# Down and output tiles of a transformer layer: two half-width passes in place of two half sums

## Time and profile before

| | |
|---|---|
| time, 3 runs | 985.96, 980.02, 984.0 us; median 984.0 us |
| the profiled execution | 981.32 us, its span 979.6 us |
| busy share of the span | PE 92%, weight loads 62%, DVE 60%, ACT 51%, POOL 33% |
| mean granted clock of TensorE | 0.978 of full |
| the chain that ended last | PE 80%, DVE 10%, ACT 5%, DMA 3% |
| matmuls of `split_product` (L987) | 984 |

### The profile page before, as it was taken

The page is one execution under the profiler, slowest core; times in us unless marked ns, Lnnn a source line. Parts: engine busy times, 40 slices in busy tenths (PEclk is TensorE's granted clock), DMA queues, the critical chain, the costliest instruction groups (busy, mean ns, idle before and its releaser), DMA issues.

```text
span 979.6 us, 19130 instructions
## 1 busy us (share of the span) xinstructions
PE 902.2 (92%) x7091; PEld 608.4 (62%) x7091; DVE 589.7 (60%) x1681; ACT 498.5 (51%) x998; POOL 319.3 (33%) x320
## 2 busy tenths in 40 slices
PE   2797999999999999999999999988989899989985
PEld 2665666666766666666666666554666566555764
DVE  7765666666666666666666666677576776621134
ACT  2432556565655555555555565566455454445110
POOL 4032234352525252525252535250212222211035
PEclk8899999999999999999999999999999999989998
DMA  9466242424242433333333334356747363335644
GB/s 293 132 191 206 64 137 80 132 87 130 88 127 92 120 98 108 105 108 106 105 106 104 113 99 131 102 143 201 195 121 207 104 188 110 106 94 162 193 135 150
DMA packets 142938, 129.08 MB, mean 132 GB/s; under 512 B 36176, under 2 KB 104368, under 8 KB 142624
## 3 DMA queue, kind: packets, MB, share of 16 engines
q1 hardware_dynamic: 142848, 127.87, 44.4%
HBM read 74.07 MB, written 53.22 MB: 130 GB/s over the span
## 4 chain that ended last, share of the span: by engine, by line
PE 80%; DVE 10%; ACT 5%; DMA 3%; issue 2%; POOL 1%; SPq 0%; POOLq 0%; DVEq 0%; ACTq 0%
PE bank L959 25%; PE bank L987 12%; PE o L1115 12%; PE s L1079 9%; PE st L1098 7%; PE bank L260 4%; PE bank L261 3%; PE bank L262 3%; DVE junk L1611 2%; PE bank L921 2%; DVE neg_pad L1627 1%; PE bank L934 1%; PE bank L938 1%; DMA inv_sums<-scratch_r 1%; ACT prob L1368 1%
## 5 line engine op out<-in xcount | busy, mean ns | idle before, releaser
L1368 ACT ACTIVATE prob<-st 128x512 f32<-128x512 f32 (+1 forms) x640 | 324.8, 554 | 262.7 <-PE st L1098 262.2
L1611 DVE CUSTOM_DVE_ANT_0 junk<-s,mask 128x128 bf16<-128x128 f32 (+3 forms) x512 | 229.2, 487 | 111.1 <-PE s L1079 110.9
L1614 DVE TENSOR_REDUCE part_max<-s 128x1 f32<-128x512 f32 x256 | 163.9, 682 | 96.0 <-PE s L1079 96.0
L1079 PE MATMUL s<-k,q 64*128 64x512 f32 (+3 forms) x768 | 151.7, 381 | 15.1 <-DVE part_max L1611 11.9
L527 POOL TENSOR_SCALAR_AFFINE_SELECT prob<-prob 128x512 f32<-128x512 f32 x128 | 83.4, 664 | 227.1 <-ACT prob L1368 226.6
L959 PE MATMUL bank<-x_hi,w_hi 64*128 64x512 f32 (+1 forms) x704 | 150.7, 415 | 2.4 <-DVE hid L1477 1.1
L1115 PE MATMUL o<-prob,v 128*32 128x512 f32 (+3 forms) x1536 | 145.4, 497 | 0.0
L1098 PE MATMUL st<-q,k 64*128 64x512 f32 (+3 forms) x768 | 130.5, 356 | 13.0 <-ACT prob L1368 12.9
L959 PE MATMUL bank<-x_lo,w_hi 64*128 64x512 f32 (+1 forms) x704 | 142.4, 391 | 0.0
L959 PE MATMUL bank<-x_hi,w_lo 64*128 64x512 f32 (+1 forms) x704 | 141.8, 389 | 0.0
L1079 PEld LDWEIGHTS s<-k,q 64*128 64x128 f32 x768 | 78.2, 185 | 61.7 <-DVE part_max L1611 32.0
(11 more groups left out here) (140 smaller groups left out, 1065.8 us busy)
## 6 DMA issues: line engine op xcount, KB each, us to landing
hid_in<-scratch_hid SPq DMA_DIRECT2D x16, 1408.0 KB, 7.2
q<-scratch_q SPq DMA_DIRECT2D x60, 200.0 KB
scratch_hid<-tanh_hid_hi SPq DMA_DIRECT2D x40, 256.0 KB, 2.1
scratch_hid<-hid_lo SPq DMA_DIRECT2D x40, 256.0 KB, 2.4
scratch_o<-o_sb SPq DMA_DIRECT2D x32, 256.0 KB
scratch_q<-proj_hi SPq DMA_DIRECT2D x30, 256.0 KB
k<-scratch_k SPq DMA_DIRECT2D x30, 192.0 KB
ctx<-scratch_o SPq DMA_DIRECT2D x16, 256.0 KB, 3.9
```

The costliest lines, as they stand in the source:

```text
L1079: pe.matmul(sb_[(p + odd) % S_BANKS][:, 0:wd], q[half, g % 2, h // 2, qt * P:(qt + 1) * P], k[half, g % 2, k0:k0 + wd], start=True, stop=T ...
L1368: nc.scalar.activation(prob[:, job % 3, h, 0:JOB_COLS[j]], st[at % ST_BANKS][:, 0:JOB_COLS[j]], ACT.Exp, scale=float(HD) ** -0.5).then_inc ...
L1611: ins = dve.tensor_tensor_reduce(junk[:, n % S_BANKS, 0:wd], bank_[:, 0:wd], mask[:, C - wd:C], 1.0, LOWEST, ALU.add, ALU.max, part[:, h, ...
L1614: ins = dve.tensor_reduce(part[:, h, qt, dst:dst + 1], bank_[:, 0:wd], AX.X, ALU.max)
```

## The change

Down 0 to 11 and out 0 to 7 no longer make half sums. In a first pass the upper 64 rows of the factors compute the left 256 columns into bank 0 while the lower 64 rows compute the right 256 columns into bank 1; then PE waits for its own first pass (`crossed`), and in the second pass the upper rows add their part to the right columns in bank 1 and the lower rows theirs to the left columns in bank 0. Each bank then holds finished columns. For a down tile that is 132 matmuls of 256 columns, each with a weight load of 128 columns, where there were 66 of 512; for an output tile 48 where there were 24.

The 12 steps of a down tile are now all used: five of two blocks and one of one block in the first pass, one of one and five of two in the second; `filled` comes in the 12th. ACT copies the right 256 columns of y and DVE the left 256; they stand after 12 steps. `tanh_y` and `gate_y` stand one step later in the output tile that follows. ACT no longer copies for an output tile; `combine` adds the bias straight from the two banks, in two instructions of 256 columns, and waits for `r2_done` of the tile before.

```diff
+COLUMNS = [slice(0, D // 2), slice(D // 2, D)]
+DOWN_STEPS = [[list(range(h, min(h + 2, NH))) for h in range(0, NH, 2)],
+              [list(range(max(h, 0), h + 2)) for h in range(-1, NH, 2)]]
+OUT_STEPS = [[[0, 1], [2, 3]]] * 2
...
+            def changing_over(key, factors, steps):
+                for cross in range(2):
+                    if cross:
+                        pe.wait_ge(crossed, CROSSED[key])
+                    for step in steps[cross]:
+                        for n in step:
+                            for m, (lhs, rhs) in enumerate(factors(n)):
+                                for odd in range(2):
+                                    i, half = odd ^ cross, head_rows(odd, HALF_ROWS)
+                                    mm = pe.matmul(bank[i][:, COLUMNS[i]], lhs[half], rhs[half, COLUMNS[i]],
+                                                   start=not cross and n == 0 and m == 0,
+                                                   stop=cross == 1 and n == steps[cross][-1][-1] and m == 2)
+                        if step is steps[cross][-1]:
+                            mm.then_inc(filled if cross else crossed, 1)
+                        yield 1
...
-            def copy_half_y(t):
+            def copy_right_y(t):
                 wait_filled(act, ("down", t, 0))
                 if t:
                     act.wait_ge(y_done, t)
-                nc.scalar.activation(yb[:, :], bank[1][:, :], ACT.Copy).then_inc(y_half, 1)
+                nc.scalar.activation(yb[:, COLUMNS[1]], bank[1][:, COLUMNS[1]], ACT.Copy).then_inc(y_right, 1)
...
-            def copy_half_out(t):
-                wait_filled(act, ("out", t, 0))
-                if t:
-                    act.wait_ge(r2_done, t)
-                nc.scalar.activation(r1[:, :], bank[1][:, :], ACT.Copy).then_inc(r_half, 1)
...
-            def add_half_y(t):
-                dve.wait_ge(y_half, t + 1)
-                dve.tensor_tensor(yb[:, :], bank[0][:, :], yb[:, :], ALU.add).then_inc(y_sum, 1)
+            def copy_left_y(t):
+                wait_filled(dve, ("down", t, 0))
+                if t:
+                    dve.wait_ge(y_done, t)
+                dve.tensor_copy(yb[:, COLUMNS[0]], bank[0][:, COLUMNS[0]]).then_inc(y_left, 1)
...
                 if t < SPLIT_OUT:
-                    dve.wait_ge(r_half, t + 1)
-                    dve.tensor_tensor(r1[:, :], bank[0][:, :], r1[:, :], ALU.add).then_inc(r1_done, 1)
-                    dve.wait_ge(r1_done, t + 1)
-                    dve.tensor_tensor(r1[:, :], r1[:, :], bias[:, :], ALU.add).then_inc(r_bias, 1)
-                    dve.wait_ge(r_bias, t + 1)
+                    for i, read in enumerate((r_left, r1_done)):
+                        dve.tensor_tensor(r1[:, COLUMNS[i]], bank[i][:, COLUMNS[i]], bias[:, COLUMNS[i]], ALU.add).then_inc(read, 1)
+                    dve.wait_ge(r_left, t + 1)
...
@@ ACT and DVE: where the pieces stand @@
-                        yield NH - ROUND_AT
+                        yield STEPS["down"] - ROUND_AT
-                    yield STEPS["down"] - NH
                     if 1 <= t <= NT // 2:
-                        yield 1
+                        yield 2
                         tanh_y(t)
-                        yield STEPS["out"] - 1
-                        copy_half_out(t - 1)
+                        yield STEPS["out"] - 2
...
-                        yield 2
+                        yield 3
                         gate_y(t)
-                        yield STEPS["out"] - 2
+                        yield STEPS["out"] - 3
                         combine(t - 1)
```

More of the change, by code:

```diff
@@ L203 @@
 BANKS, PRIOR = bank_places()
+CROSSED = {key: n + 1 for n, key in enumerate(key for key in BANKS if len(BANKS[key]) == 2)}
 def interleave(attention, background, background_first=False):
@@ L413, in layer @@
         d_zero = sem("d_zero")
[L414 to L417, removed]
+        y_right = sem("y_right")
+        y_left = sem("y_left")
+        r_left = sem("r_left")
         yt_done = sem("yt_done")
@@ L470, in read_out @@
             if kind == "down" and a < SPLIT_DOWN:
-                return (y_half, a + 1), (y_sum, a + 1)
+                return (y_left, a + 1), (y_right, a + 1)
             if kind == "out" and a < SPLIT_OUT:
-                return (r_half, a + 1), (r1_done, a + 1)
+                return (r_left, a + 1), (r1_done, a + 1)
             if kind == "hidden":
@@ L952, in hidden @@
                     if cross:
-                        pe.wait_ge(crossed, NCH * h + c + 1)
+                        pe.wait_ge(crossed, CROSSED["hidden", h, c])
                     for kt in range(KT):
@@ L996, in down @@
                 out_ = take_bank(("down", t, 0))
+                if t < SPLIT_DOWN:
+                    hi, lo = (hin[:, t % 2, j] for j in range(2))
+                    yield from changing_over(
+                        ("down", t, 0), lambda h: [(hi[:, h], dh[:, h]), (hi[:, h], dl[:, h]), (lo[:, h], dh[:, h])], DOWN_STEPS)
+                    return
                 for h in range(NH):
                     hi, lo = (hin[:, t % 2, j, h] for j in range(2))
[L999 to L1002, removed]
+                    mm = matmul_hi_lo(pe, out_[:, :], hi, lo, dh[:, h], dl[:, h], h == 0, h == NH - 1)
                     if h == NH - 1:
@@ L1011, in output @@
                 out_ = take_bank(("out", t, 0))
+                if t < SPLIT_OUT:
+                    hi, lo = ch[:, t % 3], cl[:, t % 3]
+                    yield from changing_over(
+                        ("out", t, 0), lambda kb: [(hi[:, kb], woh[:, kb]), (hi[:, kb], wol[:, kb]), (lo[:, kb], woh[:, kb])], OUT_STEPS)
+                    return
                 for kb in range(KT):
                     hi, lo = ch[:, t % 3, kb], cl[:, t % 3, kb]
[L1014 to L1017, removed]
+                    mm = matmul_hi_lo(pe, out_[:, :], hi, lo, woh[:, kb], wol[:, kb], kb == 0, kb == KT - 1)
                     if kb == KT - 1:
@@ L1239, in tanh_y @@
                 if t < SPLIT_DOWN:
-                    act.wait_ge(y_sum, t + 1)
+                    act.wait_ge(y_left, t + 1)
+                    act.wait_ge(y_right, t + 1)
                 else:
@@ L1332, in background @@
                             split_wo(kb)
-                        yield NH - KT * WO_STEPS
+                        yield STEPS["down"] - KT * WO_STEPS
                     else:
@@ L1340, in background @@
                             split_context(context_beside(t))
-                        yield NH - ROUND_AT
+                        yield STEPS["down"] - ROUND_AT
                     if t < SPLIT_DOWN:
-                        copy_half_y(t)
+                        copy_right_y(t)
                     else:
                         tanh_y(t)
-                    yield STEPS["down"] - NH
                     if 1 <= t <= NT // 2:
-                        yield 1
+                        yield 2
                         tanh_y(t)
-                        yield STEPS["out"] - 1
-                        copy_half_out(t - 1)
+                        yield STEPS["out"] - 2
                 for t in range(NT // 2, NT):
@@ L1496, in gate_y @@
                 if t < SPLIT_DOWN:
-                    dve.wait_ge(y_sum, t + 1)
+                    dve.wait_ge(y_left, t + 1)
+                    dve.wait_ge(y_right, t + 1)
                 if t >= 8:
@@ L1509, in combine @@
                 wait_filled(dve, key)
+                if t:
+                    dve.wait_ge(r2_done, t)
                 if t < SPLIT_OUT:
-                    dve.wait_ge(r_half, t + 1)
-                    dve.tensor_tensor(r1[:, :], bank[0][:, :], r1[:, :], ALU.add).then_inc(r1_done, 1)
-                    dve.wait_ge(r1_done, t + 1)
-                    dve.tensor_tensor(r1[:, :], r1[:, :], bias[:, :], ALU.add).then_inc(r_bias, 1)
-                    dve.wait_ge(r_bias, t + 1)
+                    for i, read in enumerate((r_left, r1_done)):
+                        dve.tensor_tensor(r1[:, COLUMNS[i]], bank[i][:, COLUMNS[i]], bias[:, COLUMNS[i]], ALU.add).then_inc(read, 1)
+                    dve.wait_ge(r_left, t + 1)
                 else:
-                    dve.wait_ge(r2_done, t)
                     dve.tensor_tensor(r1[:, :], bank_of(key)[:, :], bias[:, :], ALU.add).then_inc(r1_done, 1)
-                    dve.wait_ge(r1_done, t + 1)
+                dve.wait_ge(r1_done, t + 1)
                 dve.wait_ge(y_done, t + 1)
@@ L1585, in background @@
                             gate_y(t - 1)
-                        yield NH - GATE_AT
+                        yield STEPS["down"] - GATE_AT
                     if t < SPLIT_DOWN:
-                        add_half_y(t)
+                        copy_left_y(t)
                     else:
                         gate_y(t)
-                    yield STEPS["down"] - NH
                     if 1 <= t <= NT // 2:
-                        yield 2
+                        yield 3
```

(2 more changed lines are left out.)

## The result

The changed kernel took 968.56 us (median of 4 runs, 967.63 to 973.57) beside 983.12 us for the kernel before, a ratio of 0.988 (95% interval 0.9836 to 0.9924). Run once more on the chip of several experiments it took 970.07 beside 979.93, ratio 0.9893 (0.9866 to 0.992). By the ratios it is faster by 1.1 to 1.2%; the medians lie 14.6 and 9.9 us apart. The forecast was 969. The first profiled execution took 968.28 us where that of before took 981.32: −13.0.

What follows compares the result with a forecast made beforehand. From 686 to 909 us PE was taken to be held up by ACT and DVE, idle 19.1 of 223 us. Terms −18.4 −0.9 −0.5 +4.9 +2.5 +0.5 −3.0 gave −14.9: 969 us against the median, range 962 to 974.

Steps and rivals of the forecast that it cites:

- (a): Down-tile ends: readers and `filled` one step later remove 11.0 us of exponential and 4.5 of maxima waits; −18.4 us.
- (f): Wait of scores for turned maxima, 3.4 us, stays: two maxima and three small passes follow the last pair.
- (c): Ends of down tiles, out 2 and out 7: new wait for the bank, with no empty step left; +4.9 us.
- (b): Readers without additions: copies about 0.4 us, shorter `combine`; −0.9 us at down 11 and −0.5 after out 7.
- Rival (1): Bank wait at each of 20 ends costs the full 0.87 to 1.1 us: +12 more, 981 at worst; chance 0.17.
- (d): Down and output matmuls: 984 pairs of 256 columns for 492 of 512, 5 ns more per 512 columns; +2.5 us.
- Rival (2): Pairs of 256 columns don't keep 118 ns in runs of twelve; slower by 1% from 143 ns; chance 0.11.
- (e): 20 new change-overs between passes, about 7 with only transposed scores between costing 0.07 us each; +0.5 us.
- (g): Clock dips near 817 and 695 us go with their stalls, the one near 864 stays; −3.0 us, between 0 and −5.
- 12 steps of slack: SP's `load_hidden` waits for `filled` a step later, with this much slack, so DMA issue stays as before.

Runs made afterwards that it cites:

- the two experiments on place: Kernel before with only the readers' places moved: 976.96 us, ratio 0.9955; changed kernel with only the readers back at their former places: 978.71 us, ratio 0.9981.
- the old place: Changed kernel with only the readers back after 11 steps, tanh and gate one step earlier: 978.71 us beside 981.2, ratio 0.9981.
- the narrow copies: Changed kernel with both copies of y taking 32 of their 256 columns, part of the output left out: 970.97 us beside 979.93, ratio 0.9898.
- e9: Changed kernel with the last turning of maxima two slots later and hidden tile 2's load ten steps later on SP: 964.46 us beside 983.09, ratio 0.9828.
- e10: Changed kernel with only the last turning of maxima two slots later, the load as in the change: 967.3 us beside 983.09, ratio 0.9858.

## Why the prediction was right, point by point

**(a) Place.** Right. Waits for exponentials 11.0 → none in the stretch; the two experiments on place show cause and direction. What the step had wrong is that maxima would not wait at all: 2.7 us stay of them. Of these 1.3 us stand at 678.7, ahead of the first down tile, as they do at 678.0 in the kernel before; the earlier trace rows counts them among its 4.5, and no reader's place could remove them. Of the 4.5 that were to go 2.0 went (L1611 3.2 → 1.2 in the tiles), and 0.6 of another line that the forecast didn't count. On the other side the turned maxima, which (f) left as they were, waited 2.0 in 1 instead of 3.4 in 3, and each stall that went took with it the 0.11 us of a fresh load, which (c) counts and (a) doesn't. These errors are of opposite signs; that the sum came out is in part luck.

**(b) Readers.** 384 ns, 423 ns and 409 ns where I took 0.4 and 0.43: the rows with the same number of columns were the right ones. The wait of 0.94 us for down 12's bank, at 910.15 before, is gone, as forecast.

**(c) Bank wait.** Forecast +4.9 at nine places. Measured 3.0 us idle in seven, with 0.16 each in flight and 0.11 for the fresh load 4.9 us; 0.7 of it idle each at down 1 and 6, where DVE was to be late. The place is right, but the sum agrees by cancellation: the seven ends were forecast at 4.0 and took 4.9, and out 2 and out 7, forecast at 0.9, never wait. Rival (1), a full wait at each of 20 ends, falls.

**(d) Pairs.** 118 ns was right for long runs too, and +2.5 lies in the measured +1.3 (−1.4 to +3.9). Rival (2) falls. The rule of the Trainium skill that went with it ("TensorE: Matmul & The Clock Gate", "What overlaps and what doesn't"), by which a load overlaps only matmuls of other row groups, disagrees with the trace: 214 ns a pair by it, an estimate, and 118 measured.

**(e) Change-overs.** One of them in the changed kernel's timeline, in down 9 with a pair of 512 columns between the passes:

```profile
864.99 0.28 PE L999 MATMUL bank<-down_hi,hid_in 64*128 64x256 f32 x2
865.11 0.43 PE L1117 MATMUL st<-q,k 64*128 64x512 f32 x2
865.34 0.38 PE L999 MATMUL bank<-down_hi,hid_in 64*128 64x256 f32 x2
865.56 0.28 PE L999 MATMUL bank<-down_lo,hid_in 64*128 64x256 f32 x2
```

From the last pair of one pass to the second of the next it is 0.57 us, where 0.12 + 0.23 + 0.12 would do: 0.10 is lost, behind the first pair of the new pass. In down 11, with a pair of 256 columns between, the four starts are 890.66, 891.00, 891.22 and 891.34: 0.68 where 0.36 would do, 0.32 too much; 0.22 of that already lies ahead of the scores, so it is an upper bound for the change-over. Read in the same way at 19 of the 20 (the one of out 7 ran at the lower clock), ten lose nothing, six 0.09 to 0.13, two 0.26 and one 0.32: at most 1.4 us, not the 0.5 of the forecast. Its reading of rows 10 stopped one pair too early: a change-over also costs the pair behind the first.

**(g) Clock.** Near 817 and 695 the dips are gone (1.00 over 815 to 821 and over 694 to 698), and that near 864 remained near 855, as forecast. The one near 695 isn't visible in the earlier trace rows, where the prediction looks for it; it takes a shorter stretch. So does a fourth one in the kernel before, from 678, that the prediction left out:

```profile
678.00:682.00 4.00, 4.00 (x22) 3.52 (x24) 2.46 (x6) 0.82 (x2) 0.00 (x0) 0.62 0.33 71
694.00:698.00 4.00, 4.00 (x30) 1.57 (x30) 1.89 (x6) 0.25 (x1) 0.44 (x1) 0.59 1.09 320
```

The dip from 678 lasted longer in the changed kernel's profile (0.62 over 677 to 686). By length and clock the four stretches lost 7.2 us before (1.5, 1.6, 1.6 and 2.5) and the two that are left lose 5.1 (3.4 and 1.7): −2.1 in the down tiles, not −3.0. Behind them the clock went the other way in these two executions, 1.00 before and 0.91 after from 925 to 965 us. Over the repeated runs nothing can be read of the term: on the same chip the mean granted clock is 0.980 before (11 runs) and 0.9805 after (6), while single runs go from 0.974 to 0.987, so neither 0 nor −3 us is ruled out. One dip has its cause in part: near 855 to 866 it occurs only in profiles with the 2.0 us wait for the turned maxima ahead of it, and in none of the three in which that wait was taken away; but two profiles (the old place and the narrow copies) have the wait and no dip.

**What was missed.** "12 steps of slack" for `load_hidden` was true for the tile and not for what stands behind it on SP: key and query loads of the next group. Nor did the forecast see that PE, with its stalls gone, would come to those scores earlier, which is enough for a wait of 1.2 us by itself. It cost 1.1 to 3.3 us of PE's waiting, and 2.8 us of time where it could be taken away alone (e9 against e10).

Together, for the two profiled executions: from the first matmul of down 0 to that of down 12 it was 231.6 us (678.5 to 910.1) before and 218.8 (679.2 to 898.0) after, −12.8. PE's waits there went from 19.8 to 7.5 (the views' 20.1 and 8.8 less the 1.3 ahead of down 0, and before with down 12's 0.9): −12.3. They are nine fewer, each with 0.16 in flight and 0.11 for the fresh load: −2.4. Pairs +2.5, change-overs +1.4, the clock −2.1. The sum is −12.9; its pairs and change-overs are known only to 1 or 2 us, so that it agrees so closely is chance. Ahead of the down tiles the changed kernel's execution was 0.7 us later, where the two kernels do the same, and behind them 0.9 us shorter, −13.0 in all. Over the repeated runs the medians gained 10 to 15 us; the forecast of 15 is at the upper end, by the DMA's wait and the change-overs, while the errors in (a) and (c) nearly cancel.

## What to carry to other kernels

On an engine that works in written order, ask of each piece what stands behind it, and put the reader of a result behind whatever the bound engine wants next; then make it short, for the wait that comes next is for the buffer it reads. When a semaphore comes later, or an engine comes earlier to what it needs, look also at the DMA queue and at the loads that stand behind a waiting one. Cutting a matmul stream of 512 columns into 256 with twice the weight loads cost almost nothing here, which makes layouts possible that need no addition.

## What the runs showed of the hardware

Pairs of 64-row matmuls of 256 columns with a weight load of 128 columns each run at 0.118 us a pair over a run of twelve, 0.23 for 512 columns, so in near proportion to the columns. A pair behind a wait costs 0.11 us more. Where the upper and lower rows change over their columns after `crossed`, ten of 19 places lost nothing, six about 0.1 us and three up to 0.32 us. Two loads issued on SP behind one of 1408 KB took it 3.65 us, ahead of it 0.8 us. In the two profiled executions of the changed kernel the granted clock was at 1.2 GHz near 680 and 857 in both, and near 708 only in the second, behind its wait of 3.3 us. A run of the kernel before with a mean clock of 0.970 took 988.17 us, one with 0.986 took 974.83 us.
